# Three pipelined stages of a decoder kernel: the same operations in a new order on all engines

## The chip, the cores and the metric

One core of a Trainium2 chip runs the whole kernel in one launch. The metric is the device time of that launch in microseconds, the median of several runs. All data are float32.

## The reference

The reference is a decoder of four layers, each with self-attention, attention to a context and a feed-forward part, each of the twelve parts followed by a residual sum and a layer norm. `x` and the context are 128 sequences of 64 tokens with 128 features. Three of the twelve parts matter here:

- `L0_ffn`, a quantised feed-forward part. Every token is rounded to 8 bit with its own scale (127 over the largest absolute value), multiplied with a ternary 128 x 512 matrix, convolved along the sequence with three taps per channel, put through silu, rounded to 8 bit per token again, and multiplied with a ternary 512 x 128 matrix.
- `L2_xattn`, attention of one head over 128 features with padding: scores of `x` against the context, a mask made from the lengths, softmax, the context's tokens as values, one projection.
- the last step of `L3_ffn`, the combination of the slots: every token attends, in 16 heads of 8 features, to the 16 slots of its sequence, which hold the experts' outputs, followed by a projection.

Each ends with `x = layernorm(x + part)`.

## The kernel before, in words

The residual `x` stays in SBUF for the whole kernel as 128 features x 8192 tokens. Each part is a stage of its own function, and each of the three stages works on 16 tiles of 512 tokens (`NT = 16`). A tile passes through a fixed row of steps; each step is a function of the tile number and belongs to one engine: TensorE (`pe`), ScalarE (`act`), VectorE (`dve`), GpSimd (`pool`). The steps wait for one another through semaphores, and for the buffers, of which most exist twice (`t % 2`). An engine does its instructions strictly in the order in which they were issued.

That order is made by `staggered` (L162):

```
def staggered(turns, period, *steps):
    for _, j, m in sorted((m * period + place, j, m) for j, (place, _) in enumerate(steps) for m in range(turns)):
        steps[j][1](m)
```

Every step has a place, a number; tile m's step sorts at `m * period + place` among the steps of its own engine. The places set nothing but this order, and only their differences on one engine, taken with the period, count. They are written out by hand in each stage. There is no clock in it: at run time only the semaphores hold a step back.

**Quantised stage** (`quantised_ffn`, L1037, period 14.4). TensorE: `turn_tokens` (L1108, transposes the tokens into PSUM), `turn_back` (L1117, transposes the rounded ones back), `expand(0)`, `expand(1)` (L1129, each two of the four hidden blocks), `turn_hidden(0)`, `turn_hidden(1)` (L1144), `turn_hidden_back(0)`, `turn_hidden_back(1)` (L1159), `contract` (L1171), `variance` (L1177), `widen` (L1187). VectorE: `token_range` and the two `hidden_range` (L1286 to L1291: largest value, scale and its inverse), `tokens_back` (L1328), `copy_tokens` (L1336), four `side_tap` steps (L1349), `residual` (L1364), `keep_variance` (L1369), `close` (L1373). ScalarE: `quantise_tokens` (L1212), two `middle_tap` (L1225), two `silu` (L1234), two `quantise_hidden` (L1245), two `copy_hidden` (L1255), `square` (L1263), and every fourth tile `rstd` (L1270 to L1274, which loads another table of functions and then the old one again). GpSimd: two `hidden_back` (L1095), of two instructions each. Six steps share three pairs of PSUM banks in rotation (`pair`, `wait_emptied`); `contract`, `variance` and `widen` share bank 7. `turn_hidden` waits for both silus, `turn_hidden_back` for both `hidden_back`, `contract` for the `close` of the sixth tile before its own.

**Padded attention** (`padded_attention`, L2633, period 4.4). TensorE: `scores` (L2700), `turn` (L2709), `outputs` (L2721), `project_out` (L2732), `variance` (L2738). VectorE: `make_mask` (L2807, L2810), `add_mask` (L2818), `row_max` (L2825), `subtract` (L2830), `row_sum` (L2837, and the inverse, L2839), `residual` (L2844), `close` (L2849). ScalarE: `exponentials` (L2749), `copy_turned` (L2755), `copy_heads` (L2762), `square` (L2770), `rstd` (L2776, L2778). GpSimd: `weigh` (L2683). SyncE loads the values tile by tile, behind the next stage's weights.

**Combination of the slots** (`slot_combine`, L3526, period 7.8). GpSimd: `spread_k` and `spread_v` (both L3570; each writes the tile's slots as a block per head), `weigh` (L3586, multiplies the exponentials with the inverse sums). TensorE: `queries` (L3609), `scores` (L3622), `turn_values(0)`, `turn_values(1)` (L3632), `turn` (L3641), `outputs` (L3653), `project_out` (L3661), `variance` (L3665). VectorE: `row_max` (L3744), `subtract` (L3751), `row_sum` (L3759, and the inverse, L3761), `copy_heads` (L3767), `residual` (L3772), `close` (L3777). ScalarE: `copy_queries` (L3682), two `copy_values` (L3689), `exponentials` (L3695), `copy_turned` (L3701), `square` (L3708), `rstd` (L3714, L3716). The two steps that the prediction weighs most:

```
def close(t):
    dve.wait_ge(rs_ready, t + 1)
    dve.wait_ge(sq_ready, t + 1)
    dve.tensor_tensor(x_of(t), x_of(t), rs[t % 2][:], ALU.mult).then_inc(closed, 1)

def weigh(t):
    pool.wait_ge(rz_ready, t + 1)
    pool.tensor_tensor(E[u][:], E[u][:], rz[u][:]..., ALU.mult).then_inc(p_ready, 1)
```

`spread_k(t)` waits only for the scores of tile t - 2, `spread_v(t)` only for the turned values of tile t - 2. The output leaves in 16 pieces behind `close`.

## Time and profile before

| | |
|---|---|
| median of three runs | 4819.85 us (4819.84 to 4821.91) |
| the profiled execution | 4821.5 us |
| its span | 4819.6 us |
| mean granted TensorE clock | 0.962 of full speed |
| busy over the span | TensorE 92%, VectorE 71%, ScalarE 65%, GpSimd 31% |
| quantised stage, first to last instruction | 574.4 to 876.5 us |
| padded attention | 3003.0 to 3087.8 us |
| combination of the slots | 4666.1 to 4815.3 us |

The timeline rows below read: start in us from the span's start, duration in us, engine, line, operation, written tile <- read tiles, size, and `xN` where N instructions in a row were merged; in brackets how long the engine was idle before it and what ended the wait. The names leave digits out, so that `L_ffn_ps` is the PSUM tile of `L0_ffn` here. Instructions of one engine overlap by some hundredths of a microsecond. A step's cost on its engine is therefore best read from start to start.

### The profile page before, as it was taken

How to read it: one execution, taken by the hardware profiler on the slowest of the kernel's cores; microseconds unless marked ns; L12 is line 12 of the kernel's file. 1: busy time of each engine (PE TensorE's matmuls, PEld its weight loads, DVE VectorE, ACT ScalarE, POOL GpSimd, SP SyncE). 2: the span in 40 equal slices, each digit the busy share in tenths (PEclk: the TensorE clock that was granted, in tenths of full speed). 3: DMA queues.
4: the chain of work that ended last, by engine and by line, in shares of the span. 5: the costliest groups of instructions: out<-in, count | busy, mean ns of one | idle time of the engine just before them, and what ended most of it. 6: DMA issues, size and time to landing. Idle time of an engine off the chain costs nothing. (4 is left out here: it accounts for less than half of the span.)

```text
span 4819.6 us, 101682 instructions
## 1 busy us (share of the span) xinstructions
PE 4417.6 (92%) x37631; PEld 2907.1 (60%) x37631; DVE 3409.0 (71%) x5379; ACT 3123.7 (65%) x5579; POOL 1471.2 (31%) x1948
## 2 busy tenths in 40 slices
PE   8999788889969987999999999789979989999888
PEld 6767556557757764444444444467657767777665
DVE  7978777567763337889999995653349966666748
ACT  6878677567764336888888888653248844444356
POOL 3444354114407760000000000047734412222327
PEclk9999999889989999999999999899999999999999
DMA  3000000000021122000000000311130000000110
GB/s 106 3 2 3 2 1 1 1 13 3 3 63 51 52 69 84 1 1 1 1 1 1 1 1 20 110 31 53 53 104 3 3 2 1 1 2 1 57 55 36
DMA packets 124460, 119.57 MB, mean 25 GB/s; under 512 B 19536, under 2 KB 104528, under 8 KB 123216
## 3 DMA queue, kind: packets, MB, share of 16 engines
q1 hardware_dynamic: 106576, 77.38, 5.2%
...
## 5 line engine op out<-in xcount | busy, mean ns | idle before, releaser
L2683 POOL TENSOR_TENSOR L_xattn_E<-L_xattn_E,L_xattn_rz 128x256 f32<-128x256 f32 x16 | 10.2, 635 | 1277.6 <-DVE L_xattn_rz L2839 1277.6
L1759 POOL DMA_INDIRECT L_ffn_xg<-L_ffn_xrows,L_ffn_take x272 | 263.2, 968 | 281.1 <-DVE L_ffn_take L2054 198.8
L1823 PEld LDWEIGHTS L_ffn_ps<-L_ffn_early_down,L_ffn_mT 128*128 128x128 f32 x1904 | 246.8, 191 | 105.8 <-issue 79.8
L1765 POOL DMA_INDIRECT L_ffn_yrows<-L_ffn_yo,L_ffn_put x272 | 268.3, 987 | 99.8 <-issue 59.8
L1803 PE MATMUL L_ffn_ps<-L_ffn_up,L_ffn_xT 128*128 x544 | 259.2, 559 | 19.6 <-issue 8.1
L2919 POOL TENSOR_TENSOR L_xattn_E<-L_xattn_E,L_xattn_rz 128x1024 f32<-128x1024 f32 x64 | 123.7, 1932 | 471.5 <-DVE L_xattn_rz L3139 471.5
L1823 PE MATMUL L_ffn_ps<-L_ffn_early_down,L_ffn_mT 128*128 x1904 | 259.0, 276 | 2.5 <-DVE L_ffn_yo L2084 1.3
L2263 PE MATMUL L_attn_ps<-L_attn_rl,L_attn_wcv 128*128 128x512 f32 x512 | 240.6, 592 | 0.0
L2247 PE MATMUL L_attn_ps<-L_attn_mix,L_attn_wck 128*128 128x512 f32 x512 | 240.6, 592 | 0.0
L1913 ACT ACTIVATE L_ffn_mT<-L_ffn_ps 128x512 f32<-128x512 f32 x136 | 81.2, 597 | 236.9 <-PE L_ffn_ps L1812 236.9
L2073 DVE TENSOR_TENSOR L_ffn_m<-L_ffn_b,L_ffn_ps 128x512 f32<-128x512 f32 x136 | 93.6, 688 | 188.4 <-PE L_ffn_ps L1803 188.4
L2069 DVE TENSOR_TENSOR L_ffn_m<-L_ffn_sg,L_ffn_ps 128x352 f32<-128x352 f32 x136 | 70.9, 521 | 212.3 <-ACT L_ffn_sg L1903 212.3
L988 DVE TENSOR_REDUCE L_xattn_mx<-L_xattn_ps 128x16 f32<-128x1024 f32 x128 | 156.1, 1219 | 69.0 <-PE L_xattn_ps L812 69.0
L334 POOL TENSOR_TENSOR L_attn_Kbd<-L_attn_Kt,main_head_of_row 128x1024 f32<-128x1024 f32 x64 | 121.1, 1893 | 258.0 <-issue 249.5
L750 POOL TENSOR_TENSOR L_xattn_Kbd<-L_xattn_Kt,main_head_of_row 128x1024 f32<-128x1024 f32 x64 | 121.1, 1892 | 238.8 <-issue 233.1
L565 DVE TENSOR_TENSOR L_attn_ps<-L_attn_ps,L_attn_bias 128x512 f32<-128x512 f32 x256 | 164.9, 690 | 20.6 <-PE L_attn_ps L398 20.5
L1095 POOL TENSOR_SCALAR L_ffn_aq<-L_ffn_aq,L_ffn_qinv 128x512 f32<-128x512 f32 x64 | 126.9, 1997 | 165.0 <-ACT L_ffn_aq L1245 165.0
L2263 PEld LDWEIGHTS L_attn_ps<-L_attn_rl,L_attn_wcv 128*128 128x128 f32 x512 | 97.4, 190 | 122.4 <-issue 122.4
L2247 PEld LDWEIGHTS L_attn_ps<-L_attn_mix,L_attn_wck 128*128 128x128 f32 x512 | 92.7, 190 | 127.0 <-issue 92.7
L586 DVE TENSOR_REDUCE L_attn_mx<-L_attn_ps 128x16 f32<-128x1024 f32 x128 | 156.3, 1221 | 3.3
L824 PE MATMUL L_xattn_ps<-main_ident,L_xattn_E 128*128 128x128 f32 x1024 | 145.6, 281 | 14.1 <-ACT L_xattn_Qt L875 10.2
L596 DVE TENSOR_TENSOR L_attn_E<-L_attn_ps,L_attn_mx 128x1024 f32<-128x1024 f32 x128 | 156.1, 1220 | 2.3
...
## 6 DMA issues: line engine op xcount, KB each, us to landing
...
main_ctx<-in_ctxT SPq DMA_DIRECT2D x4, 1024.0 KB, 11.5
```

Of the source, the lines that this page charges most:

```text
L565: b = dve.tensor_tensor(scores if in_place else E[t % 2][:, 8 * at:8 * at + 8, :].rearrange("p (a h) k -> p a (h k)", a=2), scores, bias_s ...
L586: dve.tensor_reduce(mx[t % 2][:, 16 * half:16 * half + 16], score_rows(half, t), AX, ALU.max) \
L596: dve.tensor_tensor(E[u][:, rows, :], score_rows(half, t), mx[u][:, rows].rearrange("p (a o) -> p a o", o=1).to_broadcast([P, 16, S]), ALU ...
L824: m = pe.transpose(to[:, j * P:(j + 1) * P], E[t % 2][:, row:row + 2, :], k["ident"][:])
L988: dve.tensor_reduce(mx[t % 2][:, 16 * half:16 * half + 16], score_rows(half), AX, ALU.max) \
L1095: m = pool.tensor_scalar(aq[u][:, j, :], aq[u][:, j, :], ROUND, qinv[u][:, 1, j:j + 1], ALU.subtract, ALU.mult)
L1759: pool.indirect_dma_start(xg[t % RING][:], None, xrows, bass.IndirectOffsetOnAxis(ap=take[:, t:t + 1], axis=0)) \
L1765: pool.indirect_dma_start(yrows, bass.IndirectOffsetOnAxis(ap=put[:, t:t + 1], axis=0), yo[t % RING][:], None).then_inc(scattered[t % RING ...
L1803: g = pe.matmul(ps[u][:, 0, 0:F], xT[u][:], up[:, bass.ds(at, F)], start=True, stop=True)
L1823: g = pe.matmul(ps[1][:, 3, 0:P], mT[u][0:rows[a], a * P:(a + 1) * P], down[a][:, bass.ds(at, P)], start=(a == 0), stop=(a == FT - 1))
L2247: r = pe.matmul(ps[:, 5 + a % 2, :], wck[:, at(m)[0], a * P:(a + 1) * P], mix[:], start=True, stop=True)
L2263: r = pe.matmul(ps[:, 7, :], wcv[:, at(m)[0], a, :], rl[:, a, :], start=(a == 0), stop=(a == FT - 1))
```

## The change

Only the places change, in the calls of `staggered` of the three stages; the periods stay. No instruction, wait, buffer or transfer is added or taken away.

```
quantised_ffn
-            staggered(NT, 14.4, (33.5, hidden_back(0)), (35.7, hidden_back(1)))
+            staggered(NT, 14.4, (32.1, hidden_back(0)), (35.0, hidden_back(1)))
-            staggered(NT, 14.4, (0.8, turn_tokens), (9.9, turn_back), (13.6, expand(0)),
-                      (17.9, expand(1)), (24.8, turn_hidden(0)), (25.8, turn_hidden(1)),
-                      (34.5, turn_hidden_back(0)), (36.1, turn_hidden_back(1)), (47.2, contract),
-                      (47.3, variance), (128.1 , widen))
+            staggered(NT, 14.4, (-14.0, turn_tokens), (-4.8, turn_back), (-0.1, expand(0)),
+                      (8.2, expand(1)), (9.6, turn_hidden(0)), (13.2, turn_hidden(1)),
+                      (23.1, turn_hidden_back(0)), (27.0, turn_hidden_back(1)), (37.4, contract),
+                      (41.8, variance), (122.0, widen))
-            staggered(NT, 14.4, (3.5, quantise_tokens), (14.9, middle_tap(0)),
-                      (16.4, middle_tap(1)), (23.4, silu(0)), (23.9, silu(1)),
-                      (28.8, quantise_hidden(0)), (30.2, quantise_hidden(1)), (39.2, copy_hidden(0)),
-                      (41.4, copy_hidden(1)), (50.5, square), (57.5, rstd))
+            staggered(NT, 14.4, (15.6, quantise_tokens), (18.6, middle_tap(0)),
+                      (24.8, middle_tap(1)), (30.0, silu(0)), (30.9, silu(1)),
+                      (31.7, quantise_hidden(0)), (36.1, quantise_hidden(1)), (45.9, copy_hidden(0)),
+                      (46.0, copy_hidden(1)), (60.2, square), (70.2, rstd))
-            staggered(NT, 14.4, (0.0, lambda t: t and token_range(t)), (6.7, tokens_back), (8.7, copy_tokens),
-                      (14.5, side_tap(0, 0, c_mid, c_left)),
-                      (16.1, side_tap(0, 2, c_left, c_ready)), (17.9, side_tap(1, 0, c_mid, c_left)),
-                      (19.1, side_tap(1, 2, c_left, c_ready)), (26.6, hidden_range(0)),
-                      (27.2, hidden_range(1)), (46.6, residual), (51.4, keep_variance), (129.4, close))
+            staggered(NT, 14.4, (14.6, lambda t: t and token_range(t)), (20.2, tokens_back), (24.3, copy_tokens),
+                      (30.7, side_tap(0, 0, c_mid, c_left)),
+                      (33.1, side_tap(0, 2, c_left, c_ready)), (33.9, side_tap(1, 0, c_mid, c_left)),
+                      (34.5, side_tap(1, 2, c_left, c_ready)), (37.1, hidden_range(0)),
+                      (40.3, hidden_range(1)), (63.9, residual), (68.3, keep_variance), (145.9, close))
padded_attention
-            staggered(NT, 4.4, (9.7, weigh))
+            staggered(NT, 4.4, (90.8, weigh))
-            staggered(NT, 4.4, (0.0, scores), (12.4, turn), (13.6, outputs), (14.3, project_out),
-                      (18.1, variance))
+            staggered(NT, 4.4, (-4.9, scores), (5.4, turn), (6.6, outputs), (10.4, project_out),
+                      (18.6, variance))
-            staggered(NT, 4.4, (6.4, exponentials), (8.1, copy_turned), (11.3, copy_heads),
-                      (13.8, square), (16.1, rstd))
+            staggered(NT, 4.4, (5.4, exponentials), (11.5, copy_turned), (13.1, copy_heads),
+                      (18.5, square), (25.4, rstd))
-            staggered(NT, 4.4, (4.2, make_mask), (7.0, add_mask), (8.0, row_max), (8.4, subtract),
-                      (9.1, row_sum), (17.1, residual), (25.1, close))
+            staggered(NT, 4.4, (1.8, make_mask), (7.4, add_mask), (8.4, row_max), (10.2, subtract),
+                      (11.1, row_sum), (20.9, residual), (36.9, close))
slot_combine
-            staggered(NT, 7.8, (6.4, spread_k), (12.0, spread_v), (26.3, weigh))
+            staggered(NT, 7.8, (-56.8, spread_k), (-43.9, spread_v), (-36.8, weigh))
-            staggered(NT, 7.8, (0.0, queries), (9.6, scores), (13.0, turn_values(0)),
-                      (18.1, turn_values(1)), (24.1, turn), (27.5, outputs), (35.0, project_out),
-                      (37.1, variance))
+            staggered(NT, 7.8, (5.6, queries), (13.1, scores), (26.1, turn_values(0)),
+                      (28.0, turn_values(1)), (32.5, turn), (34.2, outputs), (41.6, project_out),
+                      (47.9, variance))
-            staggered(NT, 7.8, (5.2, copy_queries), (14.2, copy_values(0)), (19.2, copy_values(1)),
-                      (15.9, exponentials), (25.8, copy_turned), (37.2, square), (39.8, rstd))
+            staggered(NT, 7.8, (2.2, copy_queries), (18.4, copy_values(0)), (23.0, copy_values(1)),
+                      (14.3, exponentials), (25.3, copy_turned), (34.8, square), (40.6, rstd))
-            staggered(NT, 7.8, (18.1, row_max), (19.5, subtract), (23.1, row_sum), (35.5, copy_heads),
-                      (41.8, residual), (56.7, close))
+            staggered(NT, 7.8, (32.8, row_max), (35.1, subtract), (36.9, row_sum), (52.3, copy_heads),
+                      (58.0, residual), (75.0, close))
```

Sorted, this gives in the middle of each stage these turns, with how many tiles a step is behind the first one of its row in brackets (a row repeats without end, so that its last step stands ahead of its first of the next tile):

```
quantised  TensorE before: turn_tokens expand1(1) contract(3) variance(3) turn_hidden_back0(2) turn_hidden_back1(2)
                           turn_back turn_hidden0(1) turn_hidden1(1) widen(8) expand0
           TensorE after:  turn_tokens widen(9) expand1(1) contract(3) turn_hidden_back0(2) turn_back turn_hidden0(1)
                           turn_hidden_back1(2) variance(3) turn_hidden1(1) expand0
           ScalarE before: quantise_tokens square(3) silu0(1) silu1(1) copy_hidden0(2) copy_hidden1(2) rstd(3)
                           quantise_hidden0(1) middle_tap0 quantise_hidden1(1) middle_tap1
           ScalarE after:  quantise_tokens silu0(1) silu1(1) square(3) copy_hidden0(2) copy_hidden1(2)
                           quantise_hidden0(1) middle_tap0 quantise_hidden1(1) middle_tap1 rstd(3)
           VectorE before: token_range left0(1) right0(1) residual(3) left1(1) right1(1) tokens_back keep_variance(3)
                           copy_tokens hidden_range0(1) hidden_range1(1) close(8)
           VectorE after:  token_range left0(1) close(9) right0(1) left1(1) right1(1) tokens_back residual(3)
                           hidden_range0(1) copy_tokens keep_variance(3) hidden_range1(1)
padded     TensorE before: scores outputs(3) variance(4) project_out(3) turn(2)
           TensorE after:  scores turn(2) variance(5) project_out(3) outputs(2)
           ScalarE before: exponentials copy_heads(1) rstd(2) copy_turned square(1)
           ScalarE after:  exponentials copy_turned(1) rstd(4) copy_heads(1) square(2)
           VectorE before: make_mask row_sum(1) add_mask close(4) row_max residual(2) subtract
           VectorE after:  make_mask row_sum(2) add_mask(1) residual(4) row_max(1) subtract(1) close(7)
combine    GpSimd before:  spread_k weigh(2) spread_v
           GpSimd after:   spread_k weigh(2) spread_v(1)
           TensorE before: queries turn(3) scores(1) turn_values1(2) project_out(4) outputs(3) turn_values0(1) variance(4)
           TensorE after:  queries variance(5) turn(3) project_out(4) turn_values0(2) outputs(3) turn_values1(2) scores
           ScalarE before: copy_queries square(4) copy_values0(1) exponentials(1) rstd(4) copy_turned(2) copy_values1(1)
           ScalarE after:  copy_queries copy_values0(2) square(4) exponentials(1) copy_values1(2) rstd(4) copy_turned(2)
           VectorE before: row_max residual(3) subtract copy_heads(2) row_sum close(4)
           VectorE after:  row_max residual(3) subtract close(5) copy_heads(2) row_sum
```

The order of GpSimd in the two other stages is the same before and after.

## Rows read from the trace of the kernel before

**Rows 1.** Windows: us, busy time of PE, PEld, DVE, ACT, POOL (instructions), PEclk, DMA, GB/s
```profile
603.00:841.00 238.00, 206.12 (x1006) 142.45 (x1004) 180.44 (x359) 178.84 (x263) 119.31 (x61) 0.93 0.00 1
...
770.50:772.00 1.50, 1.50 (x9) 1.50 (x8) 0.29 (x3) 1.44 (x2) 0.00 (x0) 0.50 0.00 0
...
3036.00:3075.00 39.00, 38.19 (x366) 23.78 (x365) 38.31 (x91) 32.07 (x71) 6.12 (x10) 1.00 0.22 62
...
4680.00:4800.00 120.00, 103.58 (x1289) 68.95 (x1282) 102.81 (x101) 80.07 (x115) 106.95 (x46) 0.95 0.07 26
```

**Rows 2.** Timeline of GpSimd in the quantised stage: start us, us, instruction [idle before]
```profile
602.83 7.94 POOL L1095 TENSOR_SCALAR L_ffn_aq<-L_ffn_aq,L_ffn_qinv 128x512 f32<-128x512 f32 x4 [46.27 <-ACT L_ffn_aq L1245]
...
650.48 7.93 POOL L1095 TENSOR_SCALAR L_ffn_aq<-L_ffn_aq,L_ffn_qinv 128x512 f32<-128x512 f32 x4 [8.25 <-ACT L_ffn_aq L1245]
...
681.84 7.95 POOL L1095 TENSOR_SCALAR L_ffn_aq<-L_ffn_aq,L_ffn_qinv 128x512 f32<-128x512 f32 x4 [8.87 <-ACT L_ffn_aq L1245]
...
760.59 7.93 POOL L1095 TENSOR_SCALAR L_ffn_aq<-L_ffn_aq,L_ffn_qinv 128x512 f32<-128x512 f32 x4 [6.64 <-ACT L_ffn_aq L1245]
...
840.45 7.92 POOL L1095 TENSOR_SCALAR L_ffn_aq<-L_ffn_aq,L_ffn_qinv 128x512 f32<-128x512 f32 x4 [7.56 <-ACT L_ffn_aq L1245]
```

**Rows 3.** Timeline of TensorE in the quantised stage, one turn
```profile
754.05 1.94 PE L1159 MATMUL L_ffn_ps<-main_ident,L_ffn_aq 128*128 128x128 f32 x16
...
755.82 0.65 PE L1117 MATMUL L_ffn_ps<-main_ident,L_ffn_xq 128*128 128x128 f32 x4
...
756.31 1.91 PE L1144 MATMUL L_ffn_ps<-main_ident,L_ffn_c 128*128 128x128 f32 x16
...
767.93 1.05 PE L1177 MATMUL L_ffn_ps<-main_avg,L_ffn_sq 128*128 128x1 f32 x8 [1.51 <-ACT L_ffn_sq L1263]
...
768.84 3.19 PE L1159 MATMUL L_ffn_ps<-main_ident,L_ffn_aq 128*128 128x128 f32 x16
```

**Rows 4.** Timeline of VectorE in the same turn: the side taps of one half
```profile
767.13 2.81 DVE L1349 SCALAR_TENSOR_TENSOR L_ffn_c<-L_ffn_ps,L_ffn_taps,L_ffn_c 128x504 f32<-128x504 f32 x4
```

**Rows 5.** Timeline of the padded attention, weighing and closing steps
```profile
3035.18 0.61 POOL L2683 TENSOR_TENSOR L_xattn_E<-L_xattn_E,L_xattn_rz 128x256 f32<-128x256 f32 x1 [3.38 <-DVE L_xattn_rz L2839]
...
3035.37 0.97 DVE L2849 TENSOR_TENSOR main_x<-main_x,L_xattn_rs 128x512 f32<-128x512 f32 x1
...
3079.85 0.68 DVE L2849 TENSOR_TENSOR main_x<-main_x,L_xattn_rs 128x512 f32<-128x512 f32 x1
```

**Rows 6.** Timeline of GpSimd in the combination stage
```profile
4710.24 2.51 POOL L3570 TENSOR_TENSOR L_combine_Vbd<-L_combine_V,L_combine_early_diag 128x1024 f32<-128x1024 f32 x1
...
4719.47 2.47 POOL L3570 TENSOR_TENSOR L_combine_Kbd<-L_combine_K,L_combine_early_diag 128x1024 f32<-128x1024 f32 x1
...
4728.42 2.25 POOL L3586 TENSOR_TENSOR L_combine_E<-L_combine_E,L_combine_rz 128x1024 f32<-128x1024 f32 x1 [6.48 <-DVE L_combine_rz L3761]
...
4744.53 2.38 POOL L3586 TENSOR_TENSOR L_combine_E<-L_combine_E,L_combine_rz 128x1024 f32<-128x1024 f32 x1
...
4751.79 2.37 POOL L3586 TENSOR_TENSOR L_combine_E<-L_combine_E,L_combine_rz 128x1024 f32<-128x1024 f32 x1
...
4800.97 2.25 POOL L3586 TENSOR_TENSOR L_combine_E<-L_combine_E,L_combine_rz 128x1024 f32<-128x1024 f32 x1 [4.14 <-DVE L_combine_rz L3761]
```

**Rows 7.** Timeline of VectorE in the combination stage
```profile
4712.18 10.32 DVE L3777 TENSOR_TENSOR main_x<-main_x,L_combine_rs 128x512 f32<-128x512 f32 x1
...
4744.07 1.04 DVE L3777 TENSOR_TENSOR main_x<-main_x,L_combine_rs 128x512 f32<-128x512 f32 x1
...
4747.96 0.67 DVE L3767 COPY L_combine_at<-L_combine_ps 128x512 f32<-128x512 f32 x1
...
4749.20 1.22 DVE L3759 TENSOR_REDUCE L_combine_z<-L_combine_E 128x64 f32<-128x1024 f32 x1 [0.57 <-ACT L_combine_E L3695]
...
4750.92 1.45 DVE L3777 TENSOR_TENSOR main_x<-main_x,L_combine_rs 128x512 f32<-128x512 f32 x1
...
4814.56 0.69 DVE L3777 TENSOR_TENSOR main_x<-main_x,L_combine_rs 128x512 f32<-128x512 f32 x1 [2.66 <-ACT L_combine_rs L3716]
```

## The prediction

> **What bounds it now.** I read the three stages that the change touches, each by the busy times of its window first, then by its timeline, engine after engine. In all three the window shows two engines close to full [rows 1]: TensorE in the quantised stage (206 of 238 us), TensorE and VectorE in the padded attention (38.19 and 38.31 of 39.00), VectorE and GpSimd in the combination (102.81 and 106.95 of 120). So only the waits between them can be won or lost.
>
> *Quantised stage.* GpSimd's four operations of a tile begin at 602.83 for tile 0 and at 840.45 for tile 15 [rows 2]: 237.62 us for 15 turns, 15.84 each. The single turns differ: 6.64 idle + 7.93 busy = 14.57; 8.25 + 7.93 = 16.18; and 8.87 + 7.93 = 16.80 where `rstd` loads its tables. The 14.57 is a loop. `turn_hidden` starts at 756.31 [rows 3]; `hidden_range` and `quantise_hidden` follow, and GpSimd starts on the tile at 760.59, 4.28 later; with its 7.93 this is 12.2 to the tile's `turn_hidden_back`, and in TensorE's order both halves of that and `turn_back` (754.05 to 756.31, 2.26) stand ahead of the next `turn_hidden`. The 16.18 has the same loop at a lower clock: the same 16 transposes take 1.94 and, from 768.84, 3.19 (from 770.50 to 772.00 the granted clock is 0.50 [rows 1], the 1.2 of its 2.4 GHz), after a wait of 1.51 in which `variance` waited for the square of the residual of the `contract` just before it.
>
> *Padded attention.* The front waits for transfers that the change leaves alone. Afterwards ten tiles take 39.00 us, 3.90 each, both engines without a gap to speak of. `close` takes 0.97 where it overlaps GpSimd's `weigh` and 0.68 where it doesn't [rows 5].
>
> *Combination.* GpSimd does `spread_k`, `weigh`, `spread_v` in turn. V, K, W and V from 4710.24 to 4719.47 [rows 6] take 9.23: 2.45 for each of three spreads (a little under the 2.47 of the last, since they overlap) and 1.88 for the weighing, 6.78 per tile. The turns last 7.26 (4744.53 to 4751.79). The cause is `close`, the only VectorE operation here whose two inputs both lie in SBUF. At 4712.18 it takes 10.32 us [rows 7]: it stands while GpSimd runs five instructions back to back, past four boundaries between them, and ends 0.56 after the last. Later it takes 1.04 or 1.45 and gets in when the running `spread_k` ends, since the next instruction, `weigh`, only just got what it waits for (the 1/z computed immediately ahead of `close`), and `weigh` takes 2.38 in place of 1.9. I read this as: GpSimd gives way to a waiting `close` only where its next instruction was not ready early.
>
> **The change, part by part.** No instruction is added or removed; all terms are waits. The sum stands against the profiled execution, 4821.5 us (span 4819.6), 1.65 above the median 4819.85.
>
> *(a) Quantised stage, TensorE's order.* `variance` now stands behind turn_hidden_back(0), `turn_back`, turn_hidden(0) and turn_hidden_back(1), so the 1.51 idle goes. Between turn_hidden_back(0) and the next turn_hidden(0) stand half of the transposes (754.05 to 755.82 is 1.77 for all) and `turn_back` (to 756.31, 0.49): 0.88 + 0.49 = 1.4 where 2.26 stood; the loop becomes 12.2 + 1.4 = 13.6. TensorE's own work is 14.79 (754.05 to 768.84) less 1.51, 13.3, and hides under that. But another chain is late next: the side taps (2.81 for four) [rows 4], then `tokens_back` on VectorE, which `turn_back` waits for in front of turn_hidden(0); laid out on paper turn by turn, this holds turn_hidden(0) back by 0.6: 14.2 per turn. `contract` waits for the `close` of 9 tiles back, which now comes after the first side tap; in this layout it ends level with GpSimd's 7.93, cost nothing, and 0.5 if the cover is gone. `rstd` now stands behind middle_tap(1), and its tables delay both silus: 2.1 in three turns, about what it costs now (16.80 - 14.57 = 2.2). 15 x 14.2 + 3 x 2.1 = 219.3. Lower-clock stretches: now they cost 237.6 - 15 x 14.57 - 3 x 2.2 = 12.5, eight of 1.6 (16.18 - 14.57). TensorE will still be idle about 0.9 a turn, in two pieces instead of one, so between none and all eight; nearest neither, I take half, 6.3. Sum 225.6, **-12.0**, bounds -18.3 and -5.8. The other moves (ScalarE's `square` behind the silus, `copy_tokens` between the ranges) change no wait on this loop. Fill -0.7 (turn_hidden(0) no longer behind turn_back(1)), end +0.7 (variance(14) after the last transposes).
>
> *(b) Padded attention.* `weigh` now overlaps add_mask and `residual`, which read PSUM; `close` runs free: 0.97 - 0.68 = 0.29 off VectorE's 3.9, less some 0.1 because `subtract` now follows `row_max` directly. TensorE then bounds: it idles 0.81 of 39.00, 0.08 a tile, over 13 tiles 1.1; and one `variance` (0.9) moves from ahead of the last `outputs` into the wait behind it. **-2.0**, between -4 (the clock rises earlier in the front, where TensorE now has one more scores in its gap) and +1 (four closes left over at the end). `weigh` keeps its order, so 90.8 for 9.7 is nothing.
>
> *(c) Combination: GpSimd.* `spread_v` of the tile before follows `weigh`. Its inputs and buffers are free in both orders and the values are wanted a turn later: 0, bounds -1 and +1.
>
> *(d) Combination: `close` ahead of 1/z.* VectorE's order becomes row_max, residual, subtract, close, copy_heads, row_sum. From the start of `weigh` of tile t: row_max, residual and subtract of t+1 take 2.9 (4745.11 to 4747.96), so `close` asks at 2.9, while `spread_v` runs (1.9 to 4.3). The `spread_k` behind it has long been ready (its scores were done before row_max could start), so by my reading GpSimd keeps going to 6.8. There it must wait: its next `weigh` needs a 1/z that stands behind the stuck `close`. Then close (0.56), copy_heads, row_sum and reciprocal (4747.96 to 4750.92 is 2.96, of which 0.57 was waiting for the exponential, long done now: 2.39) and 0.1: 3.0 us in which GpSimd idles. A turn takes 6.8 + 3.0 = 9.8 instead of 7.26. Against it stands a better start: GpSimd will idle 3.0 behind the first stuck `close`, now 6.48, and the `spread_k` ahead of weigh(5), which now ends at 4721.94, has one `spread_v` fewer ahead of it: 4721.94 - 2.45 + 3.0 puts weigh(5) at 4722.6, where it now starts at 4728.42. From weigh(5) to weigh(13) 8 x 9.8 = 78.4; weigh(14) and weigh(15) have no `spread_k` left ahead, 7.35 each: weigh(15) at 4815.7, now 4800.97. The end behind it stays 12.0 (4803.22 to 4815.25 now): **+14.5**; bounds +10 (one or two turns escape) and +20.
>
> Sum: -12.0 - 2.0 + 0 + 14.5 = +0.5 on the profiled 4821.5; less the 1.65, the median is **4820.4**.
>
> The Trainium skill (SBUF — State Buffer, "Who interferes with whom") speaks to (d): whichever of VectorE with two SBUF inputs and a reading GpSimd op issues first has the shared pair for that whole instruction, and the other blocks. Taken as "until the running instruction ends", `close` would be let in at 4.3; the 10.32 over five instructions speaks against that, the 1.04 and 1.45 for it. What it would give is rival A.
>
> **Rivals.** *A, close gets in at each boundary.* Close asks at 2.9, starts at 4.3, GpSimd loses 0.5; 1/z comes 3.0 later: 7.35 a turn and no first stall, weigh(5) at 4720.1, weigh(15) at 4793.6: -7.4 instead of +14.5, total -21.4, **4798.5**. For it: the later closes (1.04 and 1.45) do enter at a boundary now. Against: these had a late-readied `weigh` behind the boundary; the one with ready successors stood through four. 0.18.
>
> *B, slower: TensorE's clock falls in the combination.* At 9.8 a turn TensorE idles in two waits (for copy_heads, and scores for subtract) some 3 us. Its work there is 103.58 us for 16.5 turns, 6.3 each; at half clock 12.5, which takes over as the bound once the mean clock falls below 6.3/9.8 = 0.64. Price 2.7 x 10 = 27 if it stays low, 13.5 if half of the time: **4833.9**. For it: 1.51 idle cost the clock eight times in the quantised stage by the sum of (a). Against: these waits are shorter, and the loop passes GpSimd and VectorE, not TensorE. 0.12.
>
> *C, the quantised stage doesn't gain*: the clock falls as often and `close` delays `contract`: -12.0 becomes -2, total +10.5, **4830.4**. 0.06.
>
> **Numbers.** My case 0.64. About 0.2% (9.6 us) is what a measurement of this kernel can tell from no change. My case, bounds -10 to +12, is within it in 9 of 10; A is faster; B and C are slower. Faster 0.20, same 0.61, slower 0.19. The range, 4798 to 4836, takes in my case, C, the middle of B and the upper half of A.
>
> **What would show it.** (a) turns of 14.2 between GpSimd's starts, no 1.51 ahead of L1177; wrong if 15 turns still take over 232. (b) close at 0.68 and ten tiles in under 38.5. (d) close at L3777 of about 4.5 us in every turn, GpSimd idle 3.0 ahead of each `weigh`, turns of 9.8; if closes take 2 and turns 7.35, A holds. Granted clock under 0.7 there would be B.

## The result, and the profile after

The changed kernel takes 4797.93 us (median of 6, 4791.94 to 4805.85), the kernel before 4819.85. The ratio is 0.9956, 95% interval 0.9943 to 0.9969: 15 to 27 us faster. I had forecast 4820.4 and no change. What I gave 0.18, rival A, had been worked out as 4798.5.

The profiled execution took 4791.94 (span 4790.1), 6 under the median, so what it shows beyond 22 us is its own. Between the first and the last GpSimd step named below it is 11.3 us shorter in the quantised stage, 9.4 in the padded attention and 5.1 in the combination. From each stage's first to its last instruction it is 11.2, 7.1 and 5.2, since the padded attention now closes its last tiles later; the remaining 6.0 of the 29.6 lie in stages that the change doesn't touch. Its windows of the three stages, to be held against [rows 1]: us, busy time of PE, PEld, DVE, ACT, POOL (instructions), PEclk, DMA, GB/s.

```profile
603.00:829.00 226.00, 195.06 (x1006) 130.12 (x1004) 181.18 (x358) 179.38 (x262) 118.90 (x60) 0.98 0.00 1
3016.00:3053.00 37.00, 37.00 (x373) 23.28 (x367) 35.09 (x87) 30.36 (x69) 6.14 (x10) 1.00 0.23 67
4655.00:4775.00 120.00, 111.90 (x1335) 74.65 (x1336) 107.46 (x105) 81.23 (x120) 111.62 (x48) 0.97 0.07 27
```

The quantised stage does the same 1006 matmul records in 226 us that took 238, at a granted clock of 0.98 instead of 0.93. TensorE's idle time there has hardly changed (238.00 - 206.12 = 31.9 before, 226.00 - 195.06 = 30.9 now); its busy time fell by 11.1. That is about what the clock accounts for: in the traces the granted clock was 0.50 for 34.1 us of the window before and for 10.2 us of this one, and if that time is full of matmuls, half of the difference is 12.0 us (an estimate). The timeline of GpSimd there, to be held against [rows 2]:

```profile
602.77 7.95 POOL L1095 TENSOR_SCALAR L_ffn_aq<-L_ffn_aq,L_ffn_qinv 128x512 f32<-128x512 f32 x4 [46.70 <-ACT L_ffn_aq L1245]
...
662.45 7.94 POOL L1095 TENSOR_SCALAR L_ffn_aq<-L_ffn_aq,L_ffn_qinv 128x512 f32<-128x512 f32 x4 [6.13 <-ACT L_ffn_aq L1245]
...
722.00 7.94 POOL L1095 TENSOR_SCALAR L_ffn_aq<-L_ffn_aq,L_ffn_qinv 128x512 f32<-128x512 f32 x4 [6.60 <-ACT L_ffn_aq L1245]
...
829.09 7.93 POOL L1095 TENSOR_SCALAR L_ffn_aq<-L_ffn_aq,L_ffn_qinv 128x512 f32<-128x512 f32 x4 [6.26 <-ACT L_ffn_aq L1245]
```

15 turns take 226.32 (237.62 before). Ten of them are between 14.07 and 14.54, an idle of 6.13 to 6.60 plus 7.94; the other five, the first two and those in which `rstd` loads its tables, take 15.5 to 18.1. TensorE in one turn, as [rows 3]:

```profile
772.58 3.67 PE L1171 MATMUL L_ffn_ps<-L_ffn_aT,L_ffn_early_w 128*128 128x512 f32 x8 [0.92 <-DVE main_x L1373]
776.09 1.04 PE L1159 MATMUL L_ffn_ps<-main_ident,L_ffn_aq 128*128 128x128 f32 x8
...
779.54 0.95 PE L1177 MATMUL L_ffn_ps<-main_avg,L_ffn_sq 128*128 128x1 f32 x8
```

No idle ahead of L1177 (1.51 before); instead `contract` waits 0.92 for the `close` of the sixth tile before its own, which I had taken as free. Before 705 us that wait isn't there, but 1.51 us idle stand ahead of turn_hidden_back(0) (L1159), and still the clock is full from 645 us on.

The combination, GpSimd first (against [rows 6]), then the first two closes of VectorE (against [rows 7]):

```profile
4694.76 2.96 POOL L3570 TENSOR_TENSOR L_combine_Kbd<-L_combine_K,L_combine_early_diag 128x1024 f32<-128x1024 f32 x1
4697.76 1.94 POOL L3586 TENSOR_TENSOR L_combine_E<-L_combine_E,L_combine_rz 128x1024 f32<-128x1024 f32 x1
4699.65 2.50 POOL L3570 TENSOR_TENSOR L_combine_Vbd<-L_combine_V,L_combine_early_diag 128x1024 f32<-128x1024 f32 x1
4702.11 2.95 POOL L3570 TENSOR_TENSOR L_combine_Kbd<-L_combine_K,L_combine_early_diag 128x1024 f32<-128x1024 f32 x1
4705.10 1.94 POOL L3586 TENSOR_TENSOR L_combine_E<-L_combine_E,L_combine_rz 128x1024 f32<-128x1024 f32 x1
```
```profile
4693.01 2.35 DVE L3777 TENSOR_TENSOR main_x<-main_x,L_combine_rs 128x512 f32<-128x512 f32 x1
...
4700.45 2.25 DVE L3777 TENSOR_TENSOR main_x<-main_x,L_combine_rs 128x512 f32<-128x512 f32 x1
```

`close` asks (that is, its record begins) at 4700.45 while `spread_v` runs. It ends at 4702.70, 0.55 after `spread_v`, and the `spread_k` behind takes 2.95 instead of 2.48. So it was let in at the first end of an operation, although that `spread_k` had long been ready. The turn is 7.34, not 9.8: rival A to 0.01. The old order turned in 7.26, so what is won here isn't the turn but the first close: weigh(0) to weigh(15) takes 107.92 instead of 112.99. This execution was lucky there: two more executions of the same places, in the probe kernels below, took 110.37 and 110.34, with a first close of 4.81 and 4.80.

In the padded attention, `weigh` of tile 0 to tile 15 takes 60.70 us instead of 70.12. Only 1.5 of that lies in tiles 5 to 15 (37.41 instead of 38.91, in a window where TensorE is busy all the time). The rest, 7.9, is the front, which I had left alone but for a bound.

### The profile page after: what moved, and what is told of

Its sections match the earlier page's. It is cut to its first block and busy times, and to the rows that moved or that the text cites. A ratio compares the mean times of both kernels' runs of the same rounds, so it can differ in the third digit from the quotient of the medians.

```text
span 4790.1 us, 101682 instructions
## 1 busy us (share of the span) xinstructions
PE 4402.6 (92%) x37631; PEld 2890.5 (60%) x37631; DVE 3411.8 (71%) x5379; ACT 3121.6 (65%) x5579; POOL 1474.8 (31%) x1948
## 5 line engine op out<-in xcount | busy, mean ns | idle before, releaser
L1903 ACT ACTIVATE L_ffn_sg<-L_ffn_ps 128x352 f32<-128x352 f32 x136 | 63.1, 464 | 146.3 <-PE L_ffn_ps L1805 146.3
L824 PE MATMUL L_xattn_ps<-main_ident,L_xattn_E 128*128 128x128 f32 x1024 | 144.9, 280 | 14.2 <-ACT L_xattn_Qt L875 10.3
```

The lines of the kernel that those rows point to most:

```text
L824: m = pe.transpose(to[:, j * P:(j + 1) * P], E[t % 2][:, row:row + 2, :], k["ident"][:])
```

## The experiments

"Stage time" is from the first to the last `weigh` (in the quantised stage from GpSimd's first to its sixteenth start) in the kernel's profiled execution. Ratios are to runs of the kernel before on the same chip (medians 4816 to 4818). Theories and rivals are numbered as in the expectation printed above each result; each was written before its run.

### Each stage alone

The diff above, cut to one stage at a time.

**ffn_only.** 

> Only the quantised stage has its new places; the two others are as before. Theory 1 (the parts add, each by what its stage shows in the changed kernel): GpSimd's first and sixteenth start in the stage lie 226.3 us apart (237.6 before), the kernel is 11.4 faster, median 4808.5. Since the combination is the old one, it also tells whether the long close (10.32 us) belongs to that order: theory 1 says that it comes again, about 10 us, with 13.3 between weigh(4) and weigh(5). Rival 2 (the long close was one execution's accident): all closes under 2.5 us and 7.3 between weigh(4) and weigh(5); the profiled execution is then 6 lower than 4810.

4805.18, ratio 0.9975 (0.9965 to 0.9985), that is 12 faster. Stage time 224.16. The long close came again:

```profile
4689.11 10.31 DVE L3777 TENSOR_TENSOR main_x<-main_x,L_combine_rs 128x512 f32<-128x512 f32 x1
```

It belongs to the old order: in the eight kernels with the combination unchanged it took 10.32 (before), 10.31, 10.33, 10.32, 10.33, 10.36, 10.33 and 10.33, whatever clock and stages came before.

**padded_only.** 

> Only the padded attention has its new places. In the changed kernel its weigh steps span 60.7 us from tile 0 to tile 15 in place of 70.1. Theory 1 (the order itself does this: TensorE has more work in the wait for the first context tokens, its clock rises earlier, and ten tiles take 37.4 instead of 39.0): 60.7 again, the kernel is 9.4 faster, median 4810.5. Rival 2 (the wait for the transfers fell luckily, and only the steady turns are won): 66 to 68, the kernel is 2 to 4 faster, median 4817. The long close of the combination comes again if it belongs to the old order of the combination, and doesn't if it was an accident.

4811.41, ratio 0.9986 (0.9977 to 0.9995), 7 faster. Stage time 60.83 with a 6.43 wait for the tokens still in it, so the order does it, not a lucky transfer.

**combine_only.** 

> Only the combination has its new places. Theory 1 (the old order always stalls once, the new one never): weigh(0) to weigh(15) 107.9 instead of 113.0, turns of 7.34, closes of 2.25, the kernel is 5 faster, median 4815. Rival 2 (the stall was an accident of one execution): the same turns of 7.34, but the kernel is no faster or up to 1 slower, median 4820 to 4821, since the old turns are 7.26. My prediction on record (closes that starve, turns of 9.8) would give 4834.

4811.15, ratio 0.9989 (0.9980 to 0.9998), 5 faster. Turns 7.34, closes 2.23 to 2.26, except the first:

```profile
4707.11 5.51 DVE L3777 TENSOR_TENSOR main_x<-main_x,L_combine_rs 128x512 f32<-128x512 f32 x1
```

It asked 0.04 before the end of a `weigh`, wasn't let in there nor at the end of the `spread_v` behind it (GpSimd at 4705.26, 4707.15, 4709.59, unstretched), and ended 0.55 after GpSimd had run out of work at 4712.07. Stage time 110.34. So theory 1 holds only in part: the new order doesn't always escape, but it stalls for less.

**combine_vector**, VectorE's places alone:

```
-            staggered(NT, 7.8, (18.1, row_max), (19.5, subtract), (23.1, row_sum), (35.5, copy_heads),
-                      (41.8, residual), (56.7, close))
+            staggered(NT, 7.8, (32.8, row_max), (35.1, subtract), (36.9, row_sum), (52.3, copy_heads),
+                      (58.0, residual), (75.0, close))
```

> In the combination only VectorE has its new places (close right behind subtract); GpSimd, TensorE and ScalarE keep the old ones, all else is as before. Theory 1 (VectorE's order alone decides: close asks while a spread runs and is let in at its end): closes of about 2, turns of 7.35, no stall, median 4815 as with the whole new combination. Rival 2 (what lets close in is GpSimd's or TensorE's new order): closes of 4 or more in some turns, or one of 10 again, and weigh(0) to weigh(15) over 112, median 4820 or more.

4812.51, 0.9989 (0.9980 to 0.9998); turns 7.33, closes 2.2, first close 6.65, stage time 108.72. VectorE's order alone gives the new turns; the places of the other three engines, GpSimd's among them, are worth nothing that can be seen, as (c) had it.

### Who gets in between VectorE and GpSimd

**port_probe.** Thirty trials behind the end of the changed kernel. GpSimd does a chain of spreads and weighings; VectorE's part of a trial (`go` starts the chain, `n` sets the delay):

```
+                dve.tensor_reduce(dl[:, 4 * i:4 * i + 1], k["ctx"][:, 0:8], AX, ALU.add).then_inc(go, 1)
+                n = int(d * 960)
+                m = dve.tensor_reduce(dl[:, 4 * i + 1:4 * i + 2], k["ctx"][:, 0:n], AX, ALU.add)
...
+                dve.tensor_tensor(xp[:], xp[:], ps[:] if psum else rp[:], ALU.mult).then_inc(ddone, 1)
```

> The changed kernel with 30 trials behind its end, each by itself: GpSimd runs a chain of its own operations of the combination (K a spread of 2.45 us, W a weighing of 1.9, all ready from the start), and VectorE asks with one two-input SBUF multiply of 512 columns (0.6 us when free) at 0.4 to 2.2 us after the chain's start. Theory 1 (VectorE gets in only where GpSimd's queue runs dry): in the chains of five ready instructions the multiply takes 9 to 12 us whatever the phase, and it gets in at the end of the second spread where the third instruction waits for a semaphore. Rival 2 (it gets in at the next boundary, the 10.32 has another cause): it takes 0.9 to 2.6 us, always ending 0.6 after the end of the running instruction. Rival 3 (phase decides): for the same chain some phases end at the first boundary and others pass several. Where the multiply reads one input from PSUM, theories 1 to 3 all say 0.6 to 0.7; if it is slow too, the cause isn't the shared access to SBUF.

All 28 asks with both inputs in SBUF were let in at the first end of an operation, whatever the phase and whatever stood ready behind: asked 0.3 after the start of a spread it took 2.72, at 1.2 it took 1.83, at 2.1 it took 0.93. With one input from PSUM:

```profile
4870.74 2.72 DVE L3848 TENSOR_TENSOR probe_xp<-probe_xp,probe_rp 128x512 f32<-128x512 f32 x1
...
5105.66 0.68 DVE L3848 TENSOR_TENSOR probe_xp<-probe_xp,probe_ps 128x512 f32<-128x512 f32 x1
```

So the reading on which my (d) stood, that a ready successor keeps VectorE out, is wrong for these asks, and the price hangs on both inputs lying in SBUF.

**long_probe.** The same with chains of thirteen, a semaphore at each operation, asks behind two to four operations.

```
+                    if N * i + j >= 4:
+                        pool.wait_ge(pdone, N * i + j - 3)
+                    if i % 2 and j >= 5:
+                        pool.wait_ge(rel, i // 2 + 1)
```

> The changed kernel with 24 trials behind its end. In each, GpSimd runs 13 operations of the combination back to back (spread, spread, weigh, and again), each raising a semaphore and waiting for one that was raised three operations earlier, and VectorE asks with the two-input multiply 5.0 to 9.4 us after the start, so with two to four operations behind GpSimd. In every second trial the sixth operation also waits for a semaphore that VectorE raises right before it asks, as the weighing does in the combination. Theory 1 (a multiply that asks in the middle of a long unbroken chain is passed over until the chain ends): durations of 15 us and more in the plain trials. Rival 2 (only the phase or a just-raised semaphore ahead does it): some trials pass several ends of operations, those with the late semaphore more often. Rival 3 (the port is handed over at every end, as in the short chains): all 24 end 0.6 after the end of the operation that ran when they asked, and the 10.32 stays without a cause.

Rival 3: all 24 were let in at the next end at the latest, those with the late semaphore like the others. (Six of them fell within 0.1 us of an end and took 0.68 to 0.72.)

```profile
4856.64 2.14 DVE L3840 TENSOR_TENSOR probe_xp<-probe_xp,probe_rp 128x512 f32<-128x512 f32 x1
```
```profile
4856.30 1.93 POOL L3811 TENSOR_TENSOR probe_Eo<-probe_E,main_ident 128x1024 f32<-128x1024 f32 x1
4858.19 5.36 POOL L3816 TENSOR_TENSOR probe_Ko<-main_ctx,main_ident 128x1024 f32<-128x1024 f32 x2
```

4856.64 + 2.14 is 0.55 after 4858.23, where the weighing ends, and the two spreads behind take 5.36 instead of 4.91.

**The probe kernels' own combination.** Ahead of the trials both probe kernels are the changed kernel, so they show its combination twice more. VectorE, then GpSimd, in port_probe:

```profile
4691.66 4.81 DVE L3777 TENSOR_TENSOR main_x<-main_x,L_combine_rs 128x512 f32<-128x512 f32 x1
```
```profile
4690.97 2.52 POOL L3570 TENSOR_TENSOR L_combine_Vbd<-L_combine_V,L_combine_early_diag 128x1024 f32<-128x1024 f32 x1
4693.42 2.51 POOL L3570 TENSOR_TENSOR L_combine_Kbd<-L_combine_K,L_combine_early_diag 128x1024 f32<-128x1024 f32 x1
4698.87 1.94 POOL L3586 TENSOR_TENSOR L_combine_E<-L_combine_E,L_combine_rz 128x1024 f32<-128x1024 f32 x1 [2.94 <-DVE L_combine_rz L3761]
```

The first close asks 0.69 after the start of a `spread_v`, as in the changed kernel's own profile (4693.01, with that `spread_v` at 4692.31), is passed over at its end, and gets in only when GpSimd has nothing ready: 4.81 instead of 2.35. In long_probe it asks 0.70 after and takes 4.80. So the same code, asking at the same place of the same operation, was let in once and passed over twice.

**close_later.** Old order, every close one tile later at the same place in the turn:

```
-                      (41.8, residual), (56.7, close))
+                      (41.8, residual), (64.5, close))
```

> Kernel before, but in the combination each close comes one tile later, at the same place of VectorE's turn. Theory 1 (the long first close belongs to its place in the turn, while GpSimd runs without a gap): the first close takes 10.3 again, 6.8 us later than before. Rival 2 (it was the coincidence of that one time): the first close is under 2.6, weigh(0) to weigh(15) about 107.

The stall came again, one turn later, and now also cost more behind it (turns of 8.1, stage time 124.01, 4835.6 in one run). VectorE, then GpSimd:

```profile
4718.12 10.26 DVE L3777 TENSOR_TENSOR main_x<-main_x,L_combine_rs 128x512 f32<-128x512 f32 x1
```
```profile
4716.13 2.50 POOL L3570 TENSOR_TENSOR L_combine_Vbd<-L_combine_V,L_combine_early_diag 128x1024 f32<-128x1024 f32 x1
4718.58 2.49 POOL L3570 TENSOR_TENSOR L_combine_Kbd<-L_combine_K,L_combine_early_diag 128x1024 f32<-128x1024 f32 x1
4721.02 1.95 POOL L3586 TENSOR_TENSOR L_combine_E<-L_combine_E,L_combine_rz 128x1024 f32<-128x1024 f32 x1
...
4737.80 2.25 POOL L3586 TENSOR_TENSOR L_combine_E<-L_combine_E,L_combine_rz 128x1024 f32<-128x1024 f32 x1 [9.97 <-DVE L_combine_rz L3761]
```

Theory 1: it goes with the place in the turn while GpSimd runs without a gap, not with one instant of the program.

**early_asks.** Old order, with two multiplies added on tiles of their own, behind row_max(2) and behind subtract(3):

```
+                if t == 2:
+                    dve.tensor_tensor(pr[0][:], pr[0][:], pr[1][:], ALU.mult).then_inc(probed, 1)
+                if t == 3:
+                    dve.wait_ge(probed, 3)
+                    dve.tensor_tensor(pr[0][:], pr[0][:], pr[1][:], ALU.mult).then_inc(probed, 1)
```

> Kernel before, with two added two-input multiplies on VectorE in the combination's start, on tiles of their own: behind row_max(2) and behind subtract(3), while GpSimd runs without a gap. Theory 1 (in this saturated start asks are passed over until GpSimd's queue is empty): each takes 4 us or more, and the first stretches until GpSimd waits for 1/z. Rival 2 (the first two-input operation of the stage pays, later ones don't): the first is long, the second and the first close under 2.6. Rival 3 (an end of an operation is enough, the 10.32 is a matter of phase): both under 2.6.

```profile
4689.98 2.07 DVE L3750 TENSOR_TENSOR L_combine_pr<-L_combine_pr 128x512 f32<-128x512 f32 x1
4700.93 2.70 DVE L3761 TENSOR_TENSOR L_combine_pr<-L_combine_pr 128x512 f32<-128x512 f32 x1
4711.66 1.77 DVE L3786 TENSOR_TENSOR main_x<-main_x,L_combine_rs 128x512 f32<-128x512 f32 x1
```

Each gets in at the next end (the second takes 0.10 over my 2.6). Two instructions of pure extra work made the stage 6.5 faster (106.54; 4811.71 in one run): behind them the first close no longer stalls. Rival 3, as far as an end of an operation is enough for these asks; that the phase decides about the first close is not shown, and the probe kernels' own combination speaks against it.

**close_psum.** The combination's new places, the inverse deviation left in PSUM. `close`, `residual`, `square` and `project_out` got places of their own as well, and `rstd` has no wait for an earlier `close` any more; the main lines:

```
-                    pe.wait_ge(ln_ready, t)
+                    pe.wait_ge(closed, t)
...
-                act.activation(rs[t % 2][:], rs[t % 2][:], ACT.Exp, scale=-0.5).then_inc(rs_ready, 1)
+                act.activation(ps[:, 7, :], ps[:, 7, :], ACT.Exp, scale=-0.5).then_inc(rs_ready, 1)
...
-                dve.tensor_tensor(x_of(t), x_of(t), rs[t % 2][:], ALU.mult).then_inc(closed, 1)
+                dve.tensor_tensor(x_of(t), x_of(t), ps[:, 7, :], ALU.mult).then_inc(closed, 1)
```

> Only the combination differs from the kernel before: it has the new places, and the inverse deviation is left in PSUM (ScalarE works in place in bank 7), so that close reads one input from PSUM; project_out waits for the close of the tile before, and close, residual, square and project_out have places that suit this. Theory 1 (the closes cost GpSimd 0.5 us per turn and the first stall because both inputs lie in SBUF): closes of 0.7, GpSimd without a gap, turns of 6.85, weigh(0) to weigh(15) 102 to 104 against 113.0 before and 107.9 to 110.3 with the new places alone; the kernel 8 to 10 faster than before. Rival 2 (the wait of project_out for close takes over, or VectorE does): turns of 7.3 or more, no more than 5 won.

4822.84, ratio 1.0014 (1.0005 to 1.0023): rival 2 as to the turns. The closes take 0.69 and none stalls, but the turn is 7.89. The waits of 4700 to 4790 (us in total, times, longest):

```profile
ACT L_combine_ps L3712 <- PE L_combine_ps L3665: 17.0, 12, 1.5
DVE main_x L3770 <- PE L_combine_ps L3661: 15.1, 11, 1.4
PEld L_combine_ps L3653 <- ACT L_combine_PT L3701: 13.5, 11, 1.2
POOL L_combine_E L3586 <- DVE L_combine_rz L3759: 13.0, 10, 3.5
```

ScalarE's `rstd` (L3712) waits for the variance in bank 7, `copy_turned` stands behind it and holds up `outputs`. How much of the longer turn is the bank and how much the four other places wasn't run apart.

### The front of the padded attention

TensorE in padded_only, and in combine_vector, whose padded stage is that of before, from the wait for the tokens on:

```profile
3017.27 1.97 PE L2721 MATMUL L_xattn_ps<-L_xattn_PT,L_xattn_ct 64*128 64x64 f32 x16 [6.43 <-DMA L_xattn_ct<-in_ctx_tokens]
3019.17 1.12 PE L2700 MATMUL L_xattn_ps<-main_ctx,main_x 128*64 128x64 f32 x16
```
```profile
3017.99 1.97 PE L2721 MATMUL L_xattn_ps<-L_xattn_PT,L_xattn_ct 64*128 64x64 f32 x16 [6.56 <-DMA L_xattn_ct<-in_ctx_tokens]
3020.70 2.08 PE L2732 MATMUL L_xattn_ps<-L_xattn_at,L_xattn_early_w 128*128 128x512 f32 x2 [0.75 <-ACT L_xattn_at L2762]
```

and their windows, the granted clock third from the right; two of padded_only, two of combine_vector:

```profile
3020.00:3022.00 2.00, 2.00 (x10) 0.93 (x6) 1.02 (x3) 0.63 (x2) 0.61 (x1) 0.50 0.34 98
3022.00:3024.00 2.00, 2.00 (x21) 1.38 (x22) 1.31 (x3) 0.01 (x1) 0.00 (x0) 0.71 0.37 103
```
```profile
3028.00:3030.00 2.00, 2.00 (x5) 0.76 (x3) 0.09 (x1) 1.32 (x2) 0.00 (x0) 0.50 0.34 98
3030.00:3032.00 2.00, 2.00 (x35) 1.64 (x34) 1.97 (x5) 1.30 (x3) 0.00 (x0) 0.94 0.05 9
```

In the new order `scores` stands behind `outputs`, TensorE has no gap, and the clock rises between 3022 and 3024, 6 us after the wait's end (4.4 to 5.9 in the five profiles of the new places with that wait). It had fallen in both orders already at the stage's start. In the old one `project_out` waits 0.75 for copy_heads, and it rises only at about 3030, 12 after. Of ten profiles of the old order, though, two (combine_only and ffn_pair) have a full clock from about 3021 on, 6 after the wait's end, with the same gap of 0.75, and a stage time of 67.0 instead of 70.1 to 70.5. The four windows of padded_only and combine_vector would suggest that the gap decides; these two say that it doesn't alone. From weigh(0) to weigh(3) the old order takes 23.3 to 23.7, those two 20.3, the new order 16.6 to 17.1. So some 3.0 of the front are the late clock and 3.5 are not.

**padded_project.** The old order with `project_out` behind `turn`:

```
-            staggered(NT, 4.4, (0.0, scores), (12.4, turn), (13.6, outputs), (14.3, project_out),
+            staggered(NT, 4.4, (0.0, scores), (12.4, turn), (13.6, outputs), (16.9, project_out),
```

> Kernel before, but in the padded attention TensorE does project_out behind turn instead of right behind outputs (one place). So TensorE doesn't stand 0.75 us for copy_heads after the wait for the tokens. Theory 1 (the new order wins 6.5 us in the front because TensorE runs without a gap after that wait and its clock rises 5 us later instead of 9 to 10): weigh(0) to weigh(3) falls from 23.3 to under 20, the kernel is 3 to 6 faster than before. Rival 2 (the front's gain comes from elsewhere, VectorE's or ScalarE's order): 23.3 again, no more than 1 us won.

weigh(0) to weigh(3) fell from 23.3 to 20.8, and the clock was full from 3022 on, 6 after the end of the tokens' wait at 3015.90, with a gap of 0.13. That fits theory 1's mechanism, but not its size (it said under 20), and it is no more than the old order had by itself in two profiles. But the turns became 4.50 instead of 3.89, since `residual` now waits 0.5 for `project_out` in each, and the kernel was 7 slower (1.0015, 1.0006 to 1.0024).

**tokens_before** and **tokens_after**, the edit on the kernel before and on the changed one:

```
-            for stage in ahead:
-                stage.load(sp)
             for t in range(NT):
+                if t == RING:
+                    for stage in ahead:
+                        stage.load(sp)
```

> Kernel before, but in the padded attention the first four tiles' context tokens are sent ahead of the next stage's expert weights in SyncE's queue. Theory 1 (the 6.5 us wait is these transfers queued behind the weights, and the half clock follows from the wait): the wait goes, the clock rises 6 to 12 us earlier, weigh(0) to weigh(15) falls from 70.1 to about 60, the kernel is 8 to 12 faster. Rival 2 (the transfers share the 16 engines anyway, the order in the queue hardly counts): the wait stays over 3 us and the kernel gains under 4.

> The changed kernel with the same edit: tokens ahead of the expert weights. Theory 1 (of the padded stage's 9.3 us, 6.5 come from how the two orders live through the wait for tokens, 1.5 to 2.5 from the steady turns): weigh(0) to weigh(15) about 57, 2 to 3 under that of tokens_before, and the kernel 3 to 5 faster than the changed kernel, median 4793 to 4795. Rival 2 (the new order wins by itself, wait or none): it stays 6 or more under tokens_before.

The wait for tokens is gone in both. tokens_before: 4812.43, 0.9985 (0.9976 to 0.9994), 7 faster where I expected 8 to 12, stage time 63.60; the clock still rises only 9.6 after the gap, now 0.76. In tokens_after it rises 11 after a wait of 0.57, without any gap behind it. tokens_after: 4791.70, 0.9942 (0.9928 to 0.9956), stage time 57.23. The difference of the two stage times is 6.4: rival 2, the new order wins by itself. From weigh(0) to weigh(3) they take 16.77 and 11.44, at half clock but for the last 2.1 of the former: besides the gap of 0.76, a turn of the old order holds a `variance` of 2.07 at half clock that the new order puts a tile later. The first full turns of TensorE at half clock take 7.1 and 5.3. That is the larger part of what isn't the clock's rise; the rest wasn't taken apart.

**padded_close.** The changed kernel, one place:

```
-                      (11.1, row_sum), (20.9, residual), (36.9, close))
+                      (11.1, row_sum), (20.9, residual), (33.9, close))
```

> The changed kernel, but in the padded attention close stands between add_mask and residual again instead of behind subtract. My step (b) (close overlaps weigh and takes 0.97 instead of 0.68): with TensorE as bound (turns of 3.74) the 0.3 more are hidden or cost 0.1, ten turns 37.4 to 38.5. Rival 2 (VectorE is still level with TensorE): 38.9 as before.

Ten turns 39.88, so 0.25 more per turn and not hidden: neither of the two values. The price of the overlap is paid in full, since VectorE has no slack at a turn of 3.74.

```profile
3035.10 0.97 DVE L2849 TENSOR_TENSOR main_x<-main_x,L_xattn_rs 128x512 f32<-128x512 f32 x1
```

(In the changed kernel its sixteen closes take 0.68 to 0.69.) This one place gives more than the steady gain of the stage.

### The quantised stage taken apart

**ffn_variance**, **ffn_pair** and **ffn_triple** make one, two and three of the moves on the kernel before:

```
-                      (47.3, variance), (128.1 , widen))
+                      (53.7, variance), (128.1 , widen))
```
```
-                      (27.2, hidden_range(1)), (46.6, residual), (51.4, keep_variance), (129.4, close))
+                      (27.2, hidden_range(1)), (46.6, residual), (56.9, keep_variance), (129.4, close))
-                      (41.4, copy_hidden(1)), (50.5, square), (57.5, rstd))
+                      (41.4, copy_hidden(1)), (50.5, square), (60.0, rstd))
```

> Kernel before, but in the quantised stage TensorE does variance between turn_hidden(0) and turn_hidden(1), not right behind contract (one place). Theory 1 (of the stage's 11.4 the greater part is the 1.51 wait and the clock that falls after it): no idle ahead of L1177, at most half as many low-clock stretches, GpSimd's first to sixteenth start in 228 to 232 us in place of 237.6 to 240.1, kernel 6 to 10 faster. Rival 2 (the shorter loop, with turn_hidden_back(1) behind turn_hidden(0), is what counts): 234 or more, at most 4 faster.

> Kernel before, but in the quantised stage variance stands between turn_hidden(0) and turn_hidden(1) on TensorE (as in ffn_variance) and keep_variance behind hidden_range(1) on VectorE. Theory 1 (ffn_variance was slow only because keep_variance, ahead of hidden_range in VectorE's order, waited for the late variance): the wait at L1369 goes, GpSimd's first to sixteenth start in 224 to 232 us, 6 to 12 faster than before. Rival 2 (TensorE's place for variance costs by itself, the gain came from the shorter way to the next turn_hidden): 236 or more, no gain or a loss.

> Kernel before, but in the quantised stage variance (TensorE), keep_variance (VectorE) and rstd (ScalarE, behind middle_tap(1)) all come later, as in the changed kernel; every other place is the old one. Theory 1 (the late variance needs its two followers late as well, then the wait and the loop are free): 224 to 232 us from GpSimd's first to sixteenth start, 6 to 12 faster than before. Rival 2 (these moves are no gain by themselves; what wins is turn_hidden_back(1) behind turn_hidden(0), which shortens the way from one tile's turn_hidden_back to the next tile's turn_hidden): 236 us or more.

Ratios 1.0035 (1.0022 to 1.0049), 1.0060 (1.0047 to 1.0074) and 1.0052 (1.0038 to 1.0065); stage times 255.0, 265.1 and 264.9: every step slower than before. ffn_variance removes the 1.51 in all but the last turn, and loses more in the waits of 620 to 840:

```profile
DVE L_ffn_var L1369 <- PE L_ffn_ps L1177: 42.2, 13, 4.0
ACT L_ffn_aq L1245 <- DVE L_ffn_qs L1291: 33.1, 10, 4.1
```

`keep_variance` stands ahead of `hidden_range` on VectorE, so a late `variance` holds up the loop. Moving it too (ffn_pair) removed that wait, and the stage still took longer; moving `rstd` too didn't mend it. The clock was no better for it either: 0.94, 0.93 and 0.94 from 603 to 840 us, where the kernel before has 0.93 and the changed one 0.98. So the idle I named was real, but removing it by itself wins nothing; the stage's gain needs the rest of the order, and which part of it keeps the clock up stays open. Whether that is the shorter way from turn_hidden_back(0) to the next turn_hidden(0), as I had it, wasn't run alone and stays open.

### Versions that should beat both kernels

**all_three**: changed kernel with the tokens first and close_psum's combination. 

> The changed kernel with the context tokens ahead of the expert weights and with the combination of close_psum. If the parts add: the changed kernel's 21 to 22, the tokens' 5 to 6 and the combination's 4 to 5 more give 31 to 33 under before, a ratio of 0.9933. If close_psum's gain isn't there, it equals tokens_after (0.9942).

4806.23, 0.9975 (0.9964 to 0.9985): the combination as slow as in close_psum (112.64).

**best_of**: the new places in the two first stages, tokens first, early_asks in the combination. 

> The new places in the quantised stage and in the padded attention, the context tokens ahead of the expert weights, and the old order of the combination with the two added multiplies of early_asks. Theory 1 (the early asks keep the stall away whatever the clock and the stages before did): closes of 1.5 to 1.8, weigh(0) to weigh(15) 106.5 against 107.9 to 110.4 with the new order and 113 before, the kernel 1 to 2 faster than tokens_after, ratio 0.9938 to 0.9942. Rival 2 (early_asks was luck of one execution): a close of 5 to 10 us again, 113 us, ratio 0.9952 or more.

4794.20, 0.9952 (0.9939 to 0.9966). The combination did as theory 1 said (first close 1.74, stage time 106.45, turns 7.26), the kernel's ratio did not. But tiles 5 to 15 of the padded stage took 43.47 instead of 37.41, and 43.29 in all_three. `outputs` stood still again:

```profile
3018.41 1.97 PE L2722 MATMUL L_xattn_ps<-L_xattn_PT,L_xattn_ct 64*128 64x64 f32 x16 [2.83 <-issue]
```
```profile
3010.00:3014.00 4.00, 4.00 (x41) 2.52 (x40) 3.85 (x11) 3.33 (x9) 0.61 (x1) 1.00 1.15 312
3014.00:3018.00 4.00, 1.57 (x4) 0.38 (x2) 3.51 (x9) 1.99 (x5) 0.61 (x1) 1.00 0.80 196
3018.00:3022.00 4.00, 3.59 (x35) 3.39 (x36) 0.58 (x3) 1.48 (x4) 0.00 (x0) 0.54 0.36 101
```

The profile names no releaser. 312 GB/s flowed from 3010 to 3014, and the expert weights now stand in the queue ahead of tile 4's tokens, so a late transfer of these tokens is the likely cause, but that isn't shown. Behind the gap the clock was 0.54. In tokens_after the same order of transfers cost nothing in the profiled execution. tokens_after is the fastest version measured (0.9942 against 0.9956 for the change); the intervals overlap, so that it beats the change is likely, not shown.

## Why the prediction was wrong

**The step that failed is (d).** It put "by my reading GpSimd keeps going to 6.8" and so turns of 9.8 and +14.5. The steady `close` gets in at the end of the running operation, in every turn behind the first close and in all 52 asks of the two probes; the turn is 7.34, and in place of +14.5 the stage won 5.1 in this profile, 2.6 in the probe kernels' (ratio of it alone 0.9989). The Trainium skill (SBUF — State Buffer, "Who interferes with whom") gives the pair to one instruction at a time, and read as "until the running instruction ends" it was right in those. By the trace I had one case of a ready successor, the 10.32, and raised it to a rule; the 1.04 and 1.45 were better evidence and I explained them away by a condition (the late-readied `weigh`) that no row had isolated.

**But the 10.32 is no accident** either: eight kernels repeat it to 0.05, and close_later moves it by a turn. With VectorE's new places the first close took 2.35 and 3.06 in two profiles (the changed kernel, tokens_after) and 4.80, 4.81, 5.50, 5.51 and 6.65 in five (long_probe, port_probe, padded_close, combine_only, combine_vector), each of these five ending 0.55 after the last operation that GpSimd had ready. So for the first close my reading, that it stands until GpSimd runs dry, holds in most profiles, and what failed is its extension to the others. What keeps it out is not found. It isn't readiness behind, the length of the chain or a just-raised semaphore, which didn't do it in the probes. (One difference wasn't tried: the stage's `weigh` works in place, the probes' writes another tile.) Nor does the moment of asking decide by itself: 0.7 after the start of a `spread_v` it took 2.35 once and 4.8 twice, and 0.01 to 0.04 ahead of the start of one 3.06 once and 5.5 twice. The shorter stall is what the change won in the combination, and it accounts for some of the spread between the runs.

**(a) was right in sum:** -12.0 forecast, 11.3 less by the profile, 12 by ffn_only. The terms were less good. The plain turn is 14.39 in place of 14.2 (143.86 over ten): 14.07 to 14.40 where `contract` doesn't wait for `close`, 14.53 or 14.54 in the five turns where it waits 0.92 and the clock is full. That is the 0.5 that I had named for the case that its cover is gone, and put at nothing. The clock stood at 1.00 in every 15 us stretch from 645 to 795, so the 6.3 for low-clock stretches was too much there, and by the estimate above the clock, not the shorter loop, gave most of the gain. The turns with tables took 16.2 to 18.1, two of the three more than 2.1 over the plain one. I had put the clock's fall down to the 1.51; the changed kernel keeps a 1.51 in its early turns at full clock, and ffn_variance without it stood at 0.94. And "the other moves change no wait on this loop" is wrong: in ffn_variance `keep_variance`, left in its old place, waited 42 us in all.

**(b) was mis-sized:** -2.0 forecast; 9.4 less from `weigh` to `weigh` by the profile, 7.1 less over the whole stage, 7 by padded_only. The steady turns came out as put (0.15 each). What failed is "the front waits for transfers that the change leaves alone": the transfers, yes, but TensorE stays at half clock behind the wait, and there the new order's turns are shorter (its `variance` comes a tile later) and in most profiles the clock also rises earlier. It stood there as a bound of -4, with the clock alone as its reason.

**(c) was right** as far as the times tell: combine_vector without GpSimd's move has the ratio of combine_only.

**Rivals.** A came true in the steady turns and in its total, but the total is partly luck: its "no first stall" failed in most profiles, it gave the combination -7.4 (-5.1 in the changed kernel's profile, -2.6 in the probe kernels'), and (b) was undersized by 5 to 7 the other way. B didn't occur (clock 0.97 in the combination), nor C.
